# A state-space and mixture-of-slots block on one core: logits copied and their maxima by token accumulated by VectorE in one kind of instruction

## What is computed

```python
xn = rmsnorm(x, norm_gamma)
sn = rmsnorm(slot_embeds, slot_norm_gamma)
logits = jnp.einsum('bnd,esd->bnes', xn, sn)
dispatch = jax.nn.softmax(logits, axis=1)                          # over tokens
combine = jax.nn.softmax(logits.reshape(b, n, e * s), axis=-1)     # over slots
slots = jnp.einsum('bnd,bnes->besd', xn, dispatch)
h = jax.nn.gelu(jnp.einsum('besd,edh->besh', slots, w1) + b1[None, :, None, :], approximate=False)
eo = jnp.einsum('besh,ehd->besd', h, w2) + b2[None, :, None, :]
out = jnp.einsum('bmd,bnm->bnd', eo.reshape(b, e * s, DIM), combine)
```

## Time and profile before

| | us |
|---|---|
| time, median of 3 runs | 234.22 |
| lowest and highest | 234.08, 236.19 |
| time of the profiled execution | 231.47 |
| span of the profiled execution | 229.5 |
| granted clock of TensorE over it, share of full speed | 0.993 |

### The profile page before, as it was taken

How to read it: one execution, slowest core, us unless ns; L and a number is a source line. 1 busy time by engine, 2 the same in 40 slices (tenths; PEclk the granted TensorE clock), 3 DMA queues, 4 the chain that set the end, 5 groups by cost and what they waited for, 6 DMA issues and landing times.

```text
span 229.5 us, 4239 instructions
## 1 busy us (share of the span) xinstructions
PE 208.5 (91%) x1575; PEld 150.0 (65%) x1575; DVE 138.8 (60%) x364; ACT 120.3 (52%) x264; POOL 60.8 (26%) x147
## 2 busy tenths in 40 slices
PE   3898988996789899998996799989999999999995
PEld 2544565665458695565664478776774947759995
DVE  3795869799899966878889784730040220402663
ACT  2869898531557875699530666647417053270000
POOL 6443886015632401886015610000000000000000
PEclk9999997999999999999999999999999999999999
DMA  6404000300320000000600000005222142200122
GB/s 186 118 4 140 1 0 5 94 3 0 124 106 3 0 0 0 4 0 2 188 0 1 0 3 0 0 3 171 60 57 80 49 121 64 69 26 0 49 69 69
DMA packets 15344, 10.72 MB, mean 47 GB/s; under 512 B 1773, under 2 KB 13654, under 8 KB 15326
## 3 DMA queue, kind: packets, MB, share of 16 engines
q1 hardware_dynamic: 15100, 10.31, 14.9%
q10 hardware_dynamic: 226, 0.16, 0.3%
HBM read 9.34 MB, written 1.07 MB: 45 GB/s over the span
## 4 chain that ended last, share of the span: by engine, by line
PE 71%; DVE 11%; ACT 10%; DMA 3%; issue 2%; POOL 1%; ACTq 1%; DVEq 0%
PE bank L577 30%; PE bank L922 12%; PE bank L904 11%; PE bank L761 4%; PE bank L814 3%; PE bank L750 2%; DVE xcT L1310 2%; ACT zsT L1067 2%; PE bank L829 2%; DMA vec_nat<-ffn_slot_norm_gamma_dram 1%; ACT xhT L1073 1%; PE bank L835 1%; PE bank L860 1%; PE bank L883 1%; ACT L1067 1%
## 5 line engine op out<-in xcount | busy, mean ns | idle before, releaser
L1445 DVE TENSOR_TENSOR eo<-bank,seg_e 128x512 f32<-128x512 f32 x8 | 5.5, 692 | 47.9 <-PE bank L922 47.9
L922 PEld LDWEIGHTS bank<-w_sb,zsT 128*64 128x64 f32 x256 | 27.8, 137 | 3.0 <-issue 3.0
L922 PE MATMUL bank<-w_sb,zsT 128*64 128x128 f32 x256 | 28.8, 273 | 0.0
L922 PE MATMUL bank<-w_sb,xcT 128*64 128x128 f32 x256 | 28.8, 273 | 0.0
L922 PEld LDWEIGHTS bank<-w_sb,xcT 128*64 128x64 f32 x256 | 27.8, 137 | 0.0
L904 PE MATMUL bank<-slotsT,w_sb 128*128 128x512 f32 (+1 forms) x64 | 26.1, 558 | 0.2 <-ACT zsT L1141 0.2
L1141 ACT ACTIVATE zsT<-bank,vecT 128x512 f32<-128x512 f32 x16 | 10.7, 687 | 24.9 <-PE bank L904 24.9
L577 PE MATMUL bank<-xnT,winT 128*128 128x512 f32 x48 | 23.0, 607 | 0.7 <-ACT BT L1054 0.7
L490 POOL TENSOR_TENSOR root<-root,neg_half 128x2 f32<-128x2 f32 (+1 forms) x24 | 20.3, 847 | 2.0
L904 PEld LDWEIGHTS bank<-slotsT,w_sb 128*128 128x128 f32 x64 | 11.4, 190 | 12.6 <-issue 12.1
L1310 DVE SCALAR_TENSOR_TENSOR xcT<-bank,convw,xcT 128x510 f32<-128x510 f32 (+2 forms) x24 | 17.3, 736 | 3.6 <-ACT xcT L1051 3.3
(11 more groups left out here) (165 smaller groups left out, 423.7 us busy)
## 6 DMA issues: line engine op xcount, KB each, us to landing
w_sb<-in_L_ffn_w_dram SPq DMA_DIRECT2D x16, 256.0 KB, 2.9
mods_bc<-mod_dram SPq DMA_DIRECT2D x4, 320.0 KB, 3.6
xin<-in_L_attn_x_dram SPq DMA_DIRECT2D x4, 256.0 KB, 3.1
out_dram<-x1tok SPq DMA_DIRECT2D x16, 64.0 KB, 1.5
mods_bc<-mod_dram SPq DMA_DIRECT2D x4, 192.0 KB, 3.2
seg_e<-mod_dram SPq DMA_DIRECT2D x1, 512.0 KB, 3.4
eo<-in_L_attn_in_proj_w_dram SPq DMA_DIRECT2D x1, 384.0 KB, 4.2
eo<-in_L_wmod_dram SPq DMA_DIRECT2D x1, 256.0 KB, 5.1
```

Of the source, the lines that this page charges most:

```text
L922: q = nc.tensor.matmul(o[j * S:(j + 1) * S, tile_cols(b)], act_h[j][k // 2][:, k % 2, at:at + S], w2_sb[j][:, k, :], start=k == 0 and b == ...
```

## The change

`copy_logits` on ScalarE and `token_max` on VectorE go. A new visit on VectorE, `copy_and_token_max`, stands at the turns that `token_max` had. For each of the two banks it issues one `tensor_scalar`, which multiplies the logits by 1.0, writes them to `lt_sb`, and accumulates their maximum into one column of `rshift`. Each counts up `lt_done`. The semaphore `rshift_done` goes, and `shifts` waits for `lt_done` in its place. No other turn is changed.

```diff
-        rshift_done = sem("rshift_done", 2)
...
             def shifts(bi):
                 def visit(j, it):
 
-                    wait(pe, rshift_done, j, it, bi + 1)
+                    wait(pe, lt_done, j, it, 2 * bi + 2)
 
                     wait(pe, cshift_done, j, it, bi + 1)
...
-            def copy_logits(bi):
-                def visit(j, it):
-                    for n in range(NT):
-                        wait(act, lt_ps, j, it, 2 * bi + n + 1)
-                        A(lt_sb[j][:, n, :], bank[4 * j + (2, 0)[bi] + n][:, :], ACT.Copy).then_inc(lt_done[1][j], 1)
-                return visit
...
-            def token_max(bi):
-                def visit(j, it):
-                    wait(dve, lt_done, j, it, 2 * bi + 2)
-                    with nc.allow_low_precision("the shift of a softmax"):
-                        V.reduce_max(rshift[j][:, :], lt_sb[j][:, :, :], AX.X).then_inc(rshift_done[1][j], 1)
+            def copy_and_token_max(bi):
+                def visit(j, it):
+                    for n in range(NT):
+                        wait(dve, lt_ps, j, it, 2 * bi + n + 1)
+                        with nc.allow_low_precision("the shift of a softmax"):
+                            V.tensor_scalar(lt_sb[j][:, n, :], bank[4 * j + (2, 0)[bi] + n][:, :], 1.0, None, ALU.mult, ALU.max,
+                                            accum_out=rshift[j][:, n:n + 1]).then_inc(lt_done[1][j], 1)
                 return visit
...
-                      ((49, 55, 110, 113), token_max(0)), ((51, 56, 112, 114), slot_max(0)),
-                      ((60, 62, 115, 117), norm_slots(0)), ((63, 65, 116, 119), token_max(1)),
+                      ((49, 55, 110, 113), copy_and_token_max(0)), ((51, 56, 112, 114), slot_max(0)),
+                      ((60, 62, 115, 117), norm_slots(0)), ((63, 65, 116, 119), copy_and_token_max(1)),
```

More of the change, by code:

```diff
@@ L1126, in _ @@
                       ((41, 42, 95, 98), mean_squares2(0)), ((43, 47, 96, 101), mean_squares2(1)),
-                      ((44, 48, 97, 102), copy_xn2T(0)), ((45, 49, 99, 103), copy_logits(0)),
-                      ((46, 50, 100, 104), copy_xn2T(1)), ((51, 52, 105, 106), exps(0)),
-                      ((54, 57, 107, 109), copy_logits(1)), ((55, 58, 108, 110), copy_slotsT(0)),
+                      ((44, 48, 97, 102), copy_xn2T(0)), ((46, 50, 100, 104), copy_xn2T(1)), ((51, 52, 105, 106), exps(0)),
+                      ((55, 58, 108, 110), copy_slotsT(0)),
                       ((59, 60, 111, 112), exps(1)), ((62, 67, 113, 114), copy_slotsT(1))]
```

## The result

| | before | changed |
|---|---|---|
| median, us | 233.25 (20 runs) | 235.52 (20 runs) |
| lowest and highest | 230.46, 236.19 | 233.40, 237.71 |
| ratio, 95% interval | | 1.0136 [1.0108, 1.0164] |
| span of the profiled execution | 229.5 | 233.2 |
| granted clock over it | 0.993 | 0.985 |

The changed kernel is slower. Its median is 2.3 us (1.0%) above that of the kernel before, its mean 2.7 us, and the ratio says 1.4%, some 3.2 us. Every ratio here compares only the faster executions of each kernel, those at most 1.5% above its fastest, so it can differ from what the medians give. The median is inside the range and on the side that was forecast (236.9, +1.1%). The profiled spans differ by more, 3.7 us, and the reason for that is the first thing that the profile after has to show.

The account below looks back on a forecast made before the run. The prediction took TensorE's wait for its next input as the bound. Delays from VectorE's copies, 1.73 us in pass 0 and 0.92 in pass 1, add 2.65 to 234.22, giving 236.9 us; range 234.4 to 239.4.

Parts of the forecast that it names:

- The bound: Whole kernel: TensorE, busy 208.5 of 229.5 us, is the bound; what counts is when it gets its next input.
- The price of the pair: VectorE, each unit: two fused copies with their accumulator reads last 1.46 us, between 1.28 and 1.87.
- The place of the copies: Transposes of the logits wait for copies at VectorE's old reduction turns: +1.73 us in pass 0, +0.92 in pass 1.
- The first units: Pass 0, first unit of each chain: transposes delayed by +0.71 us, then +1.24 in all.
- The second units: Pass 0, second unit of each chain: transposes delayed by 0.26 and 0.23 us more.
- the sign: Changed trace: TensorE idle before the transposes, about 1 us in each pass's first unit, 0.5 in the second; `slot_max` waiting.
- Pass 1: First unit of chain 0 in pass 1: the pair releases TensorE at 132.77 instead of 131.85, +0.92 us.
- the other three units: Rest of pass 1: copies cost nothing, hidden by TensorE's own work; with a pair of 1.87 the last costs 0.18.
- the sum: Both passes together: 1.73 + 0.92 = +2.65 us, 236.9 us on the median, 1.1% more.
- Dearer fusion: Rival: main instruction or accumulator read near the upper bound, pair of 1.87; +4.9 us, 239.1; chance 0.12.
- Relief of ScalarE: Rival: freed ScalarE sends `copy_xn2T` sooner, removing 2.8 us of transposes' waits in four places; 231.4 us; chance 0.08.
- "Same" by a cheap pair: Rival: pair near 1.28 or slack absorbs delay; +1.75 us or less, 234.2 to 236.5; chance 0.34 with fully hidden delay.

Follow-up runs that it names:

- ScalarE releases: Against the kernel before: ScalarE's copies stay and release the transposes, VectorE runs the 16 fused instructions on the SBUF copies; median 233.54 against 233.32, ratio 0.9913.
- Plain copies: Against the changed kernel: VectorE copies both banks with plain copies, then reduces separately as before; median 237.35 against 232.40 of the kernel before, ratio 1.0242.
- second units alone: Against the kernel before: only the four second units (bi = 1 of each chain and pass) have the fused copy; median 233.98 against 233.32, ratio 1.0027.
- the kernel without that one visit: Changed kernel with pass 1's first unit of chain 0 as before (ScalarE copies, VectorE reduces); median 233.72 against 233.32 of the kernel before, ratio 1.0051.
- first units alone: Against the kernel before: only the four first units (bi = 0 of each chain and pass) have the fused copy; median 234.25 against 233.32, ratio 1.0049.
- gap filled: Changed kernel with TensorE transposing eight old tiles during pass 1's first-unit wait, results overwritten; against the kernel before, ratio 1.0136, again 1.0146.
- reordered: Changed kernel with the same instructions, some VectorE visits and two TensorE transposes at other turns; median 233.35 against 232.40 of the kernel before, ratio 1.0082.

## Why the prediction was right, step by step

**The bound.** Right for the kernel before. What counts is when TensorE gets its next input, and not the two engines' shares of work: 11.9 us of VectorE instead of 9.7 cost nothing that shows when ScalarE releases. In the changed kernel VectorE's queue is the chain from 58 to 81 us. The prediction never called it the bound there, but its walk through the units follows that queue.

**The price of the pair.** I took 1.46 us with 0.04 to the release, 1.50 in all. Measured: 1.31 and 0.14, so 1.45. Both terms were off, and their errors cancelled. The read of the accumulator exists (16 reads of 86 ns), but it does not push the next main instruction back: the mains start 0.61 us apart, like two reductions. I had carried over ScalarE's spacing of 0.09, and that was wrong. The 0.04 to TensorE's start I had read off another hand-over, that of `unit2`. Plain copies have 0.15, so the 0.14 does not come from the accumulator. The chain of the kernel before has it too, behind `slot_max`, and I could have taken it from there:

```profile
77.84 1.30 DVE cshift L1408 x2
79.14 0.14 issue
79.27 0.61 PE bank L829 x8
```

**The place of the copies.** The mechanism was right, and each unit came out to 0.24 us or better (the table above). That the end of pass 0 is right to 0.08, +1.81 for 1.73, is in part luck. The first units were said to leave all of 1.24 behind them, and left 1.01 (1.06 by the kernel with the second units alone): 0.2 were taken up before the second units, by what I have not traced. The second units were said to cost 0.49, and cost 0.75 to 0.80, mainly because the 0.19 a group was missing. The two errors cancelled. TensorE's waits were 1.69, 1.16 and 0.87 us in the first units, where about 1, 0.5 and 1 were named as the sign, and VectorE's `slot_max` waited at every unit and not at the first alone. That all of pass 0's loss is passed on was right: the stretch between is 40.37 and 40.38 us.

**Pass 1.** The wait was right (+0.88 for +0.92), and the other three units cost nothing, as the kernel without that one visit shows (27.10 against 27.17). At full clock the stretch is longer by 0.82 (first units alone) or 0.71 (gap filled), so 0.1 to 0.2 are taken up by slack behind it. Queueing in all: 1.81 + 0.71 = 2.52 us, or 2.63, for 2.65.

**What the sum lacked.** The fall of TensorE's clock behind the wait in pass 1, 1.6 to 1.8 us when it happens (29.63 against 27.99 and 27.88); and 0.3 us around the span. The page of the kernel before shows a slice of lower clock near 36 us (7 tenths); I had it in front of me and did not ask what a longer wait would do to it. The two terms known for every execution, 2.5 + 0.3, are 2.8 us. The whole change is 2.3 us by the medians, 2.7 by the means and 3.2 by the ratio, so the clock need not have added much, and how much it did is not shown: 11 of 20 executions of the changed kernel had a mean granted clock below 0.988, but so had 16 of 75 of the kernel before, without this wait. That the forecast of 236.9 lies 1.4 above the measured median is for 1.0 us the base: the three runs before had 234.22, the twenty 233.25.

**The rivals.** Dearer fusion: ruled out, 1.31. (Its walk has a slip of 0.02: the steps behind the first are 2.06, 2.73 and 3.37, and the +4.9 stays.) Relief of ScalarE: the waits of the transposes for it are gone from the changed kernel, except one of 1.4 us on the weight loads, but longer ones for VectorE stand in their place. Its price of 2.8 us was too high from the start, since it counted each of two waits twice, for the matmuls (1.2) and for their weight loads (1.6). "Same" by a cheap pair: the pair was cheap, nearly at the lower bound, and the loss came all the same, since the release took 0.10 more and the transposes of the second units 0.19 each.

## What to carry to other kernels

A copy out of a bank that releases TensorE belongs on the engine that is free at that moment, not on the one that can do a second job with it: read what stands in front of the instruction in its engine's queue before asking what it costs. If the copy and its reduction are fused, move the visit to where its operands are ready; in the trace of this kernel that took back 2.0 of 2.5 us, and in the medians some 1.3 of 2.3. Where a change lengthens a wait of TensorE, look at the granted clock of the stretch behind it in several executions, for one profile can hold a fall that only some of them have.

## What the runs showed of the hardware

- VectorE's `tensor_scalar` with an accumulated maximum shows as `TENSOR_SCALAR_CACHE_REDUCE` (687 ns for 512 values from a bank, 682 from SBUF) and `DVE_READ_ACCUMULATOR` (86 ns, under the next instruction). A plain copy of the same bank is 684 ns.
- TensorE's clock was at half for some microseconds in 12 of 13 profiles (0.50 in a window of 2 us), and not at the same places in each; the mean granted clock was below 0.999 in 59 of 75 executions of the kernel before and in 19 of 20 of the changed one. The stretch in pass 0, behind a wait of 1.9 us, was at half clock in 7 of 13 profiles; that in pass 1, behind the wait that the change brings, in 2 of 2 of the changed kernel, but in none of the three other kernels with such a wait. What it cost differed from place to place: 1.6 to 1.8 us in pass 1, but 0.7 in pass 0 (changed kernel, 32.87 against 32.22) or 0.9 (31.31, ScalarE releasing, against 30.41 before).
- The 16 executions of the kernel before at full clock (0.999 or 1.0) have a mean of 230.7 us; the three of the changed and the filled kernel 233.7, so +3.0, with no fall of the clock in it. Three executions on different chips do not tell this from the 2.8 of the sum.
- The time around the span was 2.0 us in the median for the kernel before and for those that still had a reduction over 1,024 values on VectorE, and 2.3 to 2.4 for those that had none (changed, filled, reordered, ScalarE releasing). It is part of the loss, 0.3 us, and it is not explained.
